# Aggregating both tiles of a pair in one run over four PSUM banks, in a four-layer graph network

## The chip, the cores and the metric

The kernel runs on one core of a Trainium2 chip. The metric is device time in microseconds (us) of the whole program, lower is better. Engines: TensorE (PE), VectorE (DVE), ScalarE (ACT), GpSimd (POOL), and SyncE (SP), which here only issues DMAs. Each engine runs its own instructions in order; semaphores order them against each other.

## What is computed

`x` is 128 graphs of 64 nodes with 512 features, fp32. Each of four layers ends in `x = layernorm(x + layer(x))`. The change is in layer 1, a graph attention with four heads, an output attention and a feed-forward part:

```python
Wh = einsum('bnf,hfo->bhno', x, W_heads)                       # 4 heads, 512 -> 512
e = leaky(Wh . a[:, :O] (i)  +  Wh . a[:, O:] (j));  attn = softmax(where(adj > 0, e, -1e9))
h = elu(einsum('bhnm,bhmo->bhno', attn, Wh))  -> [b, n, 4 * 512]
out = elu(the same attention with one head, W_out [2048, 512])
y = layernorm(relu(out @ w1 + b1) @ w2 + b2 + out)
```

## The kernel before

Two graphs make a tile of 128 rows, two tiles (j = 0, 1) a pair; layer 1 takes 32 pairs. Large products are done in three passes on fp32r halves (hi and lo). The node sums come first, the weights after: for two heads at a time (q = 0, 1) PE aggregates, `agg = xa^T x attention` (`aggregate`, L2031: sixteen matmul records of 64 rows, one graph in each half of the array), ACT copies the hi half out of PSUM (`y_hi`, L1440), DVE the lo half (`y_lo`, L1737), PE projects head h (`project`, L2048, 48 matmuls into `hp`), ACT and DVE make elu (`exp` L1447, `elu` L1745 and L1748) and split it (`h_hi` L1452, `h_lo` L1754), and PE adds the head's share of the output weights into `wop` (`out_part`, L2062, 24 matmuls a head, four parts c).

Two attentions go beside it. `at` is the head attention of the next pair's tiles 2p+2 and 2p+3. Its vectors f are 8 dot products a tile: POOL multiplies (`products_of`, L1293, through only two buffers), ACT sums (`dots`, L1432). POOL makes a diagonal (`pool_diag`, L203 the large step), PE spreads it (`pe_scores`, L212), DVE does five steps (`dve_before_exp`, L221 to L234), ACT the exponential (L241), DVE `dve_after_exp`, POOL the probabilities (`pool_prob`, two parts of L254), PE turns them (`pe_turn`, L262), ACT copies (`act_turned`). `ao` is the output attention of the pair before (m = p - 1): `keep_wo` (ACT, L1460) takes `wop` out of PSUM, `out_f` (DVE, L1768 and L1772) makes two sums, POOL the diagonal (L93), then scores (PE, L101), DVE, ACT, DVE, `pool_prob`, `pe_turn` (L148), `out_sums` (L2070), `out_exp`, `out_elu` (L1778, L1781), `split_att` (ACT L1472, POOL L1298 and L1303), `natural` (DVE, L1790) and stores by SP.

PSUM has eight banks: `agg` two, `hp` two, `wop` two, `smallp` and `shared` one each; the last two hold the small products of both attentions. There is one diagonal buffer for the heads, so `pool_diag` of a tile waits until the scores of the tile before are done:

```python
pool.wait_ge(self.f_ready[j], 8 * p + HEADS)
ge(pool, self.scores_done, t)
```

The order on every engine is written out by hand in one `step(p)` for each. PE's before is: `project` 0, `out_part(m,3)` c 0 and 1, `aggregate(p,1,0)`, c 2 and 3, `project` 1, `at` turn 2p+2, `out_part(p,0)` 0 and 1, `ao` scores 2m, `aggregate(p,1,1)`, 2 and 3, `at` scores 2p+3, `project` 2, `ao` turn 2m, `out_part(p,1)` 0 and 1, `at` turn 2p+3, 2, `ao` scores 2m+1, 3, `out_sums` 2m, `aggregate(p+1,0,0)`, `project` 3, `ao` turn 2m+1, `out_part(p,2)` 0 and 1, `aggregate(p+1,0,1)`, 2 and 3, `out_sums` 2m+1, `at` scores 2p+4.

Of the kernel before, what the change touches and what calls it, by code (L numbers as in the profile page):

```python
# [160 lines left out]
class HeadAttention:  # L161
# [55 lines left out]
    def dve_before_exp(self, nc, dve, t, p, j, fill):  # L217
        dve.wait_ge(self.scores_done, t + 1)
# [4 lines left out]
                                ).then_inc(self.summed, 1)  # L223
        dve.wait_ge(self.summed, t + 1)
# [185 lines left out]
def gnn_stack_kernel(nc, x, x_turned, adj, W0T, b0, Wh, ah, Wo, ao, w1, b1, w2, b2, gamma, beta,  # L410
# [17 lines left out]
    with ExitStack() as top:  # L428
# [520 lines left out]
        with ExitStack() as ctx:  # L949
# [32 lines left out]
            smallp = pb("smallp", [P, D])  # L982
            shared = pb("shared", [P, D])
# [151 lines left out]
            def _(sp):  # L1135
# [40 lines left out]
                def step(p):  # L1176
                    if pair(p - 2):
                        store(2 * p - 3, 1)
# [3 lines left out]
                    if fresh(p + 2) and later(p):  # L1182
                        load_dots(2 * p + 4)
# [93 lines left out]
            def _(pool):  # L1277
# [30 lines left out]
                def step(p):  # L1308
                    m = p - 1
                    if pair(p + 1):  # L1310
                        if later(p):
                            products_of(2 * p + 3, p + 1, 1, range(2, 4))
                        at.pool_prob(nc, pool, 2 * p + 2)
                        if later(p):
                            products_of(2 * p + 3, p + 1, 1, range(4, 5))
                    if pair(p - 2):
                        split_att(2 * (p - 2) + 1, 1)
                    if pair(p + 1):
                        if later(p):
                            products_of(2 * p + 3, p + 1, 1, range(5, 6))  # L1320
                        at.pool_diag(nc, pool, 2 * p + 3, p + 1, 1, i64)
                        if later(p):
                            products_of(2 * p + 3, p + 1, 1, range(6, 7))
                    if pair(m):
                        ao_.pool_diag(nc, pool, 2 * m, i64)
                    if pair(p + 1):
                        if later(p):
                            products_of(2 * p + 3, p + 1, 1, range(7, NV))
                    if fresh(p + 2):
                        products_of(2 * p + 4, p + 2, 0, range(0, 2))  # L1330
                    if pair(m):
# [90 lines left out]
            def _(act):  # L1422
# [890 lines left out]
```

## Time and profile before

| | us |
|---|---|
| median of 3 runs (3083.88 to 3086.51) | 3086.3 |
| profiled execution, whole | 3088.17 |
| its span, first to last instruction | 3086.5 |

The comparison is by the median; rows of the trace add up to the span, 1.7 us less than the profiled execution's own time.

### The profile page before, as it was taken

The numbers are of one execution on the slowest core, as the hardware profiler recorded it, in microseconds if no ns is written. First come the engines' busy times: TensorE is split into PE (matmuls) and PEld (weight loads), VectorE is DVE, ScalarE is ACT, GpSimd is POOL, SyncE is SP. The second block draws the span as 40 slices with busy tenths as digits, with TensorE's granted clock in tenths as the row PEclk, the third lists the DMA queues.
The fourth block names the chain that finished last, engine by engine and source line by source line (L and its number), as shares of the span: only waits on it lengthen the run. The fifth ranks groups of instructions, "written<-read, shape, count | busy, mean of one in ns | idle before, by whom it ended". The sixth has DMA issues, their size and how long they took to land.

```text
span 3086.5 us, 65234 instructions
## 1 busy us (share of the span) xinstructions
PE 3025.1 (98%) x19324; PEld 2655.5 (86%) x19324; DVE 2321.6 (75%) x4877; ACT 1726.6 (56%) x4250; POOL 2120.1 (69%) x2901
## 2 busy tenths in 40 slices
PE   8999989999999999999999999999799999999997
PEld 7888878888998988888889888898688888888885
DVE  7777646777777777777777777675788888888885
ACT  3333335555555555555555555553577677776675
POOL 5666645666676666667666666651588888888885
PEclk9999989999999999999999999999999999999999
DMA  5555421112111111211111111112623333233220
GB/s 201 181 187 177 154 83 32 52 44 54 38 54 48 51 51 44 54 38 54 48 48 54 44 50 42 54 45 71 189 90 102 93 101 94 89 99 102 92 75 32
DMA packets 308643, 247.65 MB, mean 80 GB/s; under 512 B 150060, under 2 KB 215644, under 8 KB 308316
## 3 DMA queue, kind: packets, MB, share of 16 engines
q1 hardware_dynamic: 296796, 221.64, 24.1%
q10 hardware_dynamic: 9216, 16.78, 1.4%
q0 software_dynamic: 2560, 8.39, 0.8%
q8 instruction: 32, 0.52, 0.1%
q14 instruction: 39, 0.32, 0.0%
HBM read 162.83 MB, written 83.91 MB: 80 GB/s over the span
## 4 chain that ended last, share of the span: by engine, by line
PE 79%; issue 3%; POOL 3%; DVE 1%; DMA 0%; ACT 0%; SPq 0%; POOLq 0%; DVEq 0%; ACTq 0%
PE hp L2048 24%; PE wop L2062 23%; PE wop L47 9%; PE hp L2188 5%; PE hp L47 5%; PE agg L2031 5%; PE shared L2070 2%; PE shared L2155 2%; PE agg L2155 2%; PE shared L262 1%; POOL g_terms L1361 1%; POOL cols L403 0%; PE smallp L212 0%; PE smallp L101 0%; POOL x1b L1374 0%
## 5 line engine op out<-in xcount | busy, mean ns | idle before, releaser
L1293 POOL TENSOR_TENSOR w_first<-xd,v_row 128x512 f32<-128x512 f32 x480 | 690.9, 1452 | 351.1 <-DMA xd<-x_scratch 275.8
L2048 PE MATMUL hp<-yT_hi,big_hi 128*128 128x256 f32 x2048 | 583.7, 285 | 1.4 <-DVE yT_lo L1737 1.4
L2048 PE MATMUL hp<-yT_hi,big_lo 128*128 128x256 f32 x2048 | 580.7, 284 | 0.0
L2048 PE MATMUL hp<-yT_lo,big_hi 128*128 128x256 f32 x2048 | 580.4, 283 | 0.0
L2062 PE MATMUL wop<-big_hi,hT_hi 128*128 128x512 f32 x1024 | 424.7, 415 | 0.0
L1754 DVE TENSOR_TENSOR hT_lo<-ex,hT_hi 128x512 fp32r<-128x512 f32 x256 | 258.6, 1010 | 200.9 <-ACT hT_hi L1452 198.3
L2062 PE MATMUL wop<-big_hi,hT_lo 128*128 128x512 f32 x1024 | 401.5, 392 | 0.0
L2062 PE MATMUL wop<-big_lo,hT_hi 128*128 128x512 f32 x1024 | 400.0, 391 | 0.0
L2048 PEld LDWEIGHTS hp<-yT_hi,big_hi 128*128 128x128 f32 x2048 | 393.5, 192 | 6.8 <-DVE yT_lo L1737 1.7
L2048 PEld LDWEIGHTS hp<-yT_lo,big_hi 128*128 128x128 f32 x2048 | 393.6, 192 | 1.2
L2048 PEld LDWEIGHTS hp<-yT_hi,big_lo 128*128 128x128 f32 x2048 | 393.6, 192 | 0.0
L1432 ACT ACTIVATE w_first<-w_first 128x512 f32<-128x512 f32 x480 | 301.6, 628 | 121.1 <-POOL w_first L1293 121.1
L1361 POOL TENSOR_TENSOR g_terms<-x,g_v_row 128x512 f32<-128x512 f32 x256 | 342.3, 1358 | 35.2 <-ACT x L1613 35.2
L1737 DVE TENSOR_TENSOR yT_lo<-agg,yT_hi 128x512 fp32r<-128x512 f32 x256 | 176.3, 689 | 202.2 <-ACT yT_hi L1440 199.0
L1440 ACT CAST yT_hi<-agg 128x512 fp32r<-128x512 f32 x256 | 149.8, 585 | 262.8 <-PE agg L2031 131.1
L2062 PEld LDWEIGHTS wop<-big_hi,hT_lo 128*128 128x128 f32 x1024 | 192.2, 188 | 43.4
L2062 PEld LDWEIGHTS wop<-big_hi,hT_hi 128*128 128x128 f32 x1024 | 192.5, 188 | 42.2
L47 PE MATMUL wop<-w_hi,g_agg_hi 128*128 128x512 f32 x512 | 219.3, 428 | 4.7 <-DVE g_agg_lo L1879 4.5
L2062 PEld LDWEIGHTS wop<-big_lo,hT_hi 128*128 128x128 f32 x1024 | 193.2, 189 | 31.9
L1447 ACT ACTIVATE ex<-hp 128x512 f32<-128x512 f32 x256 | 152.9, 597 | 109.2 <-PE hp L2048 108.1
L47 PE MATMUL wop<-w_hi,g_agg_lo 128*128 128x512 f32 x512 | 202.3, 395 | 0.0
L47 PE MATMUL wop<-w_lo,g_agg_hi 128*128 128x512 f32 x512 | 201.3, 393 | 0.0
(215 smaller groups left out, 8009.2 us busy)
## 6 DMA issues: line engine op xcount, KB each, us to landing
x0f<-in_x_turned SPq DMA_DIRECT2D x64, 256.0 KB, 2.7
xt<-in_x SPq DMA_DIRECT2D x64, 256.0 KB, 3.0
x_scratch<-w_first ACTq DMA_DIRECT2D x64, 256.0 KB, 2.3
xa<-x_scratch SPq DMA_DIRECT2D x64, 256.0 KB, 2.7
att_hi_scratch<-att_hi SPq DMA_DIRECT2D x64, 256.0 KB, 2.0
att_lo_scratch<-who SPq DMA_DIRECT2D x64, 256.0 KB, 2.0
att_hi<-att_hi_scratch SPq DMA_DIRECT2D x64, 256.0 KB, 3.6
att_lo<-att_lo_scratch SPq DMA_DIRECT2D x64, 256.0 KB, 4.3
```

Source lines behind the costliest of these rows:

```text
L47: ins = nc.tensor.matmul(out, a, b, start=first and c == 0 and q == 0, stop=last and c == n - 1 and q == 2)
L1293: nc.gpsimd.tensor_tensor(terms[:, k % TR, :], xd[:], v_row[:, k, :], ALU.mult).then_inc(terms_ready, 1)
L1361: nc.gpsimd.tensor_tensor(g.terms[:, k, :], x, g.v_row[:, k, :], ALU.mult).then_inc(g.terms_ready, 1)
L1432: nc.scalar.activation(terms[:, k % TR, :], terms[:, k % TR, :], ACT.Identity, accum_out=at.f[:, j, k:k + 1]).then_inc(at.f_ready[j], 1)
L1440: nc.scalar.copy(yT[0][:, side, :, own].rearrange("p c (g n) -> p g c n", g=2), agg[:].rearrange("p g (h c n) -> p h g c n", h=2, c=KC)[:, ...
L1447: nc.scalar.activation(ex[half][:], hp[half][:], ACT.Exp).then_inc(ex_ready, 1)
L1737: nc.vector.tensor_tensor(yT[1][:, side, :, own].rearrange("p c (g n) -> p g c n", g=2), agg[:].rearrange("p g (h c n) -> p h g c n", h=2, ...
L1754: nc.vector.tensor_tensor(hT[1][:, own, :].rearrange("p c n -> p (c n)"), ex[half][:], hT[0][:, own, :].bitcast(F32).rearrange("p c n -> p ...
L2031: ins = nc.tensor.matmul(by_head(agg[:, g, :])[:, :, c, :], xa[j][own, c * P:(c + 1) * P], at.turned[own, j, 2 * q:2 * q + 2, :], start=Tr ...
L2048: ins = nc.tensor.matmul(hp[half][:, s * 2 * P:(s + 1) * 2 * P], a, b, start=c == 0 and i == 0, stop=c == KC - 1 and i == 2)
L2062: ins = nc.tensor.matmul(wop[j][:], a, b, start=h == 0 and c == 0 and i == 0, stop=h == HEADS - 1 and c == KC - 1 and i == 2)
L2188: ins = nc.tensor.matmul(bank[:, s * 2 * P:(s + 1) * 2 * P], x, y, start=c == 0 and q == 0, stop=c == KC - 1 and q == 2)
```

## The change

`smallp` and `shared` become the two banks of one tile `agg_b`. `aggregate` now does both tiles of a pair in one run, tile 0 into `agg` and tile 1 into `agg_b`. Before the second half PE waits until the small results in `agg_b` have been read, and `banks_free` makes it wait for all four `y_lo` before the next small product. The small products stand in the gaps between runs, the scores of the output attention between the halves of `project`, which is split. All orders are rewritten: on POOL and ACT the products and dots of tiles 2p+4 and 2p+5 are both made in step p (before: 2p+3 and 2p+4), `dve_before_exp` of tile 2p+3 is split in two, and SP loads for the dots earlier. The diff, shortened: indentation is cut, "..." stands for removed lines of the old orders and for unchanged bodies.

```diff
@@ -215,12 +215,18 @@
         ins.then_inc(self.scores_done, 1)
     def dve_before_exp(self, nc, dve, t, p, j, fill):
+        self.dve_add(nc, dve, t, p, j)
+        self.dve_peak(nc, dve, t, fill)
+    def dve_add(self, nc, dve, t, p, j):
...
+    def dve_peak(self, nc, dve, t, fill):
         dve.wait_ge(self.summed, t + 1)
         nc.vector.scalar_tensor_tensor(self.e1, self.e1, SLOPE_L1, self.e1, ALU.mult, ALU.max
                            ).then_inc(self.leaky, 1)
@@ -979,8 +985,10 @@
 agg = pb("agg", [P, 2, D])
 hp = [pb(f"hp{b}", [P, D]) for b in range(2)]
 wop = [pb(f"wop{j}", [P, D]) for j in range(2)]
-smallp = pb("smallp", [P, D])
-shared = pb("shared", [P, D])
+agg_b = pb("agg_b", [P, 2, D])
+shared, smallp = agg_b[:, 0, :], agg_b[:, 1, :]
+banks = (agg, agg_b)
+EVICTED = ((0, 0), (1, 0), (0, 1), (1, 1))
 SO, SH, ST = NODES, P, 3 * P
 at.prob = sb("ah_prob", [P, HEADS, 2, NODES])
 at.scores_psum = smallp[:, SH:SH + HEADS * NODES]
@@ -1174,22 +1182,21 @@
                          ).then_inc(att_stored, 16)
     def step(p):
+        if fresh(p + 2) and later(p):
+            load_dots(2 * p + 4)
         if pair(p - 2):
+            store_natural(2 * p - 4, 0)
             store(2 * p - 3, 1)
         for j in range(2):
             if pair(p) and pair(p + 1):
                 load_agg(p, j)
-        if fresh(p + 2) and later(p):
-            load_dots(2 * p + 4)
+        if fresh(p + 2):
+            load_dots(2 * p + 5)
         if isinstance(p, int) and p == PAIRS - 1:
             sp.wait_ge(at.prob_ready, T)
             sp.dma_start(w_first[:], chunked(w1)).then_inc(w_first_loaded, 16)
         if pair(p - 1):
             store_halves(2 * p - 2, 0)
-        if fresh(p + 2):
-            load_dots(2 * p + 5)
-        if pair(p - 1) and not (isinstance(p, int) and p == PAIRS - 1):
-            store_natural(2 * p - 2, 0)
@@ -1307,47 +1314,44 @@
     def step(p):
         m = p - 1
+        first = 2 * p + 4, p + 2, 0
+        second = 2 * p + 5, p + 2, 1
         if pair(p + 1):
...
+            at.pool_diag(nc, pool, 2 * p + 3, p + 1, 1, i64)
+        if fresh(p + 2):
+            products_of(*first, range(0, 1))
         if pair(p - 2):
             split_att(2 * (p - 2) + 1, 1)
+        if fresh(p + 2):
+            products_of(*first, range(1, 2))
         if pair(p + 1):
...
+            at.pool_prob(nc, pool, 2 * p + 2)
+        if fresh(p + 2):
+            products_of(*first, range(2, 4))
         if pair(m):
             ao_.pool_diag(nc, pool, 2 * m, i64)
...
         if fresh(p + 2):
...
+            products_of(*first, range(4, 6))
         if pair(m):
             ao_.pool_prob(nc, pool, 2 * m)
+        if fresh(p + 2):
+            products_of(*first, range(6, NV))
+        if pair(p + 2):
+            at.pool_diag(nc, pool, 2 * p + 4, p + 2, 0, i64)
+        if pair(m):
+            ao_.pool_diag(nc, pool, 2 * m + 1, i64)
         if pair(p + 1):
             at.pool_prob(nc, pool, 2 * p + 3)
         if fresh(p + 2):
...
+            products_of(*second, range(0, 2))
         if pair(m):
             ao_.pool_prob(nc, pool, 2 * m + 1)
         if fresh(p + 2):
...
+            products_of(*second, range(2, 5))
         if pair(m):
             split_att(2 * m, 0)
...
+        if fresh(p + 2):
+            products_of(*second, range(5, NV))
@@ -1432,13 +1436,15 @@
-    def y_hi(p, q, j, side):
+    def y_hi(p, q, n):
+        j, side = EVICTED[n]
         act.wait_ge(agg_done, 4 * p + 2 * q + j + 1)
         ge(act, h_done, 2 * (4 * p + 2 * q + side - 1))
-        ge(act, y_lo_ready, 2 * (4 * p + 2 * q + j) + side)
+        if n > 1:
+            act.wait_ge(y_lo_ready, 4 * (2 * p + q) + n - 1)
         own = slice(j * P, (j + 1) * P)
         nc.scalar.copy(yT[0][:, side, :, own].rearrange("p c (g n) -> p g c n", g=2),
-                       agg[:].rearrange("p g (h c n) -> p h g c n", h=2, c=KC)[:, side]
+                       banks[j][:].rearrange("p g (h c n) -> p h g c n", h=2, c=KC)[:, side]
                        ).then_inc(y_hi_ready, 1)
@@ -1474,122 +1480,90 @@
     def step(p):
         m = p - 1
         k = 4 * p
...
+        first = 2 * p + 4, p + 2, 0
+        second = 2 * p + 5, p + 2, 1
         if pair(m):
             h_hi(k - 1, 1)
         if pair(p - 2):
             out_exp(2 * (p - 2) + 1)
...
+        exp(k, 0)
         if pair(p + 1):
             at.act_exp(nc, act, 2 * p + 2)
...
+        if fresh(p + 2):
+            dots(*first, (0,))
         if pair(p - 2):
             split_att(2 * (p - 2) + 1, 1, p - 1)
...
+        exp(k, 1)
+        h_hi(k, 0)
+        if fresh(p + 2):
+            dots(*first, (1, 2))
+        if pair(m):
+            keep_wo(m, 0)
+        h_hi(k, 1)
+        if pair(m):
+            keep_wo(m, 1)
+        if fresh(p + 2):
+            dots(*first, (3,))
+        exp(k + 1, 0)
+        if fresh(p + 2):
+            dots(*first, (4,))
+        if pair(m):
+            ao_.act_exp(nc, act, 2 * m)
+        exp(k + 1, 1)
+        for n in range(3):
+            y_hi(p, 1, n)
         if pair(p + 1):
...
+            at.act_exp(nc, act, 2 * p + 3)
+        y_hi(p, 1, 3)
+        h_hi(k + 1, 0)
+        if fresh(p + 2):
+            dots(*first, (5, 6))
+        h_hi(k + 1, 1)
         if pair(p + 1):
             at.act_turned(nc, act, 2 * p + 2, p + 1, 0, agg_done)
...
         if pair(m):
             ao_.act_turned(nc, act, 2 * m)
         if fresh(p + 2):
...
+            dots(*first, (7,))
+        exp(k + 2, 0)
+        if pair(m):
+            ao_.act_exp(nc, act, 2 * m + 1)
+        if fresh(p + 2):
+            dots(*second, (0,))
...
@@ -1731,12 +1705,13 @@
 @block.vector
 def _(dve):
-    def y_lo(p, q, j, side):
-        dve.wait_ge(y_hi_ready, 2 * (4 * p + 2 * q + j) + side + 1)
+    def y_lo(p, q, n):
+        j, side = EVICTED[n]
+        dve.wait_ge(y_hi_ready, 4 * (2 * p + q) + n + 1)
         own = slice(j * P, (j + 1) * P)
         nc.vector.tensor_tensor(
             yT[1][:, side, :, own].rearrange("p c (g n) -> p g c n", g=2),
-            agg[:].rearrange("p g (h c n) -> p h g c n", h=2, c=KC)[:, side],
+            banks[j][:].rearrange("p g (h c n) -> p h g c n", h=2, c=KC)[:, side],
             yT[0][:, side, :, own].bitcast(F32).rearrange("p c (g n) -> p g c n", g=2),
             ALU.subtract).then_inc(y_lo_ready, 1)
@@ -1798,72 +1773,54 @@
             natural(2 * (p - 2), 0)
         if pair(p + 1):
             at.dve_before_exp(nc, dve, 2 * p + 2, p + 1, 0, fill1)
...
         if pair(p - 2):
             out_elu(2 * (p - 2) + 1)
+        elu(k, 0)
         if pair(p + 1):
             at.dve_after_exp(nc, dve, 2 * p + 2)
...
+        elu(k, 1)
+        h_lo(k, 0)
+        if pair(p + 1):
+            at.dve_add(nc, dve, 2 * p + 3, p + 1, 1)
         if pair(m):
             out_f(2 * m, 0)
         if pair(p - 2):
             natural(2 * (p - 2) + 1, 1)
...
+        h_lo(k, 1)
         if pair(m):
             ao_.dve_before_exp(nc, dve, 2 * m, fill1)
...
+        elu(k + 1, 0)
+        if pair(p + 1):
+            at.dve_peak(nc, dve, 2 * p + 3, fill1)
         if pair(m):
             ao_.dve_after_exp(nc, dve, 2 * m)
...
+        elu(k + 1, 1)
+        for n in range(4):
+            y_lo(p, 1, n)
+        h_lo(k + 1, 0)
+        if pair(m):
+            out_f(2 * m + 1, 1)
         if pair(p + 1):
             at.dve_after_exp(nc, dve, 2 * p + 3)
...
+        h_lo(k + 1, 1)
+        elu(k + 2, 0)
         if pair(m):
             ao_.dve_before_exp(nc, dve, 2 * m + 1, fill1)
...
+        elu(k + 2, 1)
+        if pair(m):
+            ao_.dve_after_exp(nc, dve, 2 * m + 1)
             out_elu(2 * m)
...
+        h_lo(k + 2, 0)
+        h_lo(k + 2, 1)
+        elu(k + 3, 0)
+        elu(k + 3, 1)
         if pair(p + 1):
...
+            for n in range(4):
+                y_lo(p + 1, 0, n)
+        h_lo(k + 3, 0)
+    for n in range(4):
+        y_lo(0, 0, n)
     dve.wait_ge(a_loaded, 16)
     run(dve, step, first=0)
@@ -2021,33 +1978,40 @@
 @block.tensor
 def _(pe):
...
+    def aggregate(p, q, before):
+        a = 2 * p + q
+        for j in range(2):
+            pe.wait_ge(at.turned_ready, 2 * (2 * p + j + 1))
+            pe.wait_ge(xa_loaded[j], 16 * p + 16)
+            ge(pe, y_lo_ready, 4 * a - 1 + j)
+            if j == 1:
+                before()
...
+            ins.then_inc(agg_done, 1)
+    def banks_free(p, q):
+        pe.wait_ge(y_lo_ready, 4 * (2 * p + q) + 4)
+    def project(p, h, half):
         k = 4 * p + h
         side = h % 2
...
+        if half == 0:
+            pe.wait_ge(y_lo_ready, 4 * (2 * p + h // 2) + 2 + 2 * side)
+        ge(pe, hv_ready, 2 * (k - 1) + half + 1)
...
@@ -2073,79 +2037,72 @@
     def step(p):
         m = p - 1
...
+        def scores_read():
+            pe.wait_ge(at.summed, capped(2 * p + 4, T))
+            if pair(m):
+                ge(pe, att_ready, 2 * (p - 2) + 2)
+                pe.wait_ge(ao_.summed, 2 * m + 1)
+        def turned_read():
+            if pair(m):
+                pe.wait_ge(ao_.turned_ready, 2 * (2 * m + 2))
+        project(p, 0, 0)
+        project(p, 0, 1)
+        if pair(m):
+            for c in range(KC):
+                out_part(m, 3, c)
         if pair(p + 1):
...
+            at.pe_scores(nc, pe, 2 * p + 3, same_graph)
+        project(p, 1, 0)
+        if pair(m):
+            pe.wait_ge(at.summed, capped(2 * p + 4, T))
+            ao_.pe_scores(nc, pe, 2 * m, same_graph)
+        project(p, 1, 1)
+        aggregate(p, 1, scores_read)
+        for c in range(KC):
+            out_part(p, 0, c)
+        banks_free(p, 1)
+        if pair(p + 1):
             at.pe_turn(nc, pe, 2 * p + 2, ident)
...
+        if pair(m):
             ao_.pe_turn(nc, pe, 2 * m, ident)
...
+        project(p, 2, 0)
+        if pair(m):
+            pe.wait_ge(ao_.turned_ready, 2 * (2 * m + 1))
+            ao_.pe_scores(nc, pe, 2 * m + 1, same_graph)
+        project(p, 2, 1)
+        if pair(m):
+            pe.wait_ge(at.turned_ready, capped(2 * (2 * p + 3), 2 * T))
+            out_sums(2 * m, 0)
+        for c in range(KC):
+            out_part(p, 1, c)
+        if pair(m):
+            pe.wait_ge(ao_.summed, 2 * m + 2)
+            ao_.pe_turn(nc, pe, 2 * m + 1, ident)
+            pe.wait_ge(att_ready, 2 * m + 1)
         if pair(p + 1):
             at.pe_turn(nc, pe, 2 * p + 3, ident)
...
+        project(p, 3, 0)
+        project(p, 3, 1)
         if pair(p + 1):
...
+            aggregate(p + 1, 0, turned_read)
+        for c in range(KC):
+            out_part(p, 2, c)
         if pair(p + 1):
...
+            banks_free(p + 1, 0)
+        if pair(m):
             out_sums(2 * m + 1, 1)
         if pair(p + 2):
...
             at.pe_scores(nc, pe, 2 * p + 4, same_graph)
...
+    def nothing_before():
+        pass
+    aggregate(0, 0, nothing_before)
+    banks_free(0, 0)
     at.pe_scores(nc, pe, 2, same_graph)
...
     run(pe, step, first=0)
```

## Rows read from the trace of the kernel before

**Rows 1.** The page's busy table: us (share of the span), instructions.

```profile
PE 3025.1 (98%) x19324; PEld 2655.5 (86%) x19324; DVE 2321.6 (75%) x4877; ACT 1726.6 (56%) x4250; POOL 2120.1 (69%) x2901
```

**Rows 2.** Windows, layer 1: length, busy us of PE, PEld, DVE, ACT, POOL; granted clock.

```profile
431.70:2140.00 1708.30, 1706.91 (x12175) 1533.19 (x12175) 1246.31 (x2306) 953.23 (x2335) 1100.13 (x1093) 1.00 0.17 47
```

**Rows 3.** The chain that ended last: start us, us, what.

```profile
1002.37 5.95 PE hp L2048 x48
...
1056.34 5.95 PE hp L2048 x48
```

**Rows 4.** Timeline of PE around one aggregation run.

```profile
1010.57 0.39 PE L2062 MATMUL wop<-big_lo,hT_hi 128*128 128x512 f32 x1
1010.79 0.39 PE L2062 MATMUL wop<-big_hi,hT_lo 128*128 128x512 f32 x1
1011.11 1.16 PE L2031 MATMUL agg<-ah_turned,xa 64*128 64x128 f32 x16
1012.20 0.50 PE L2062 MATMUL wop<-big_hi,hT_hi 128*128 128x512 f32 x1
1012.54 0.39 PE L2062 MATMUL wop<-big_lo,hT_hi 128*128 128x512 f32 x1
```

**Rows 5.** The run's first four matmuls: ns shortest/median/longest, start us.

```profile
L2031 PE MATMUL agg<-ah_turned,xa x4: 272/322/373, 1011.1 to 1011.3; 64*128 64x128 f32 x4
```

**Rows 6.** Timeline of PE: project 1 behind out_part(m,3), and the ao scores.

```profile
1028.72 0.28 PE L2048 MATMUL hp<-yT_hi,big_hi 128*128 128x256 f32 x1
...
1037.66 0.33 PE L101 MATMUL smallp<-ao_diag,same_graph 128*128 128x64 f32 x2
```

**Rows 7.** Timelines of ACT and DVE behind out_part(m,3).

```profile
1029.06 0.59 ACT L1460 COPY who<-wop 128x512 f32<-128x512 f32 x1 [1.71 <-PE wop L2062]
...
1030.81 0.69 DVE L1768 CUSTOM_DVE_ANT_0 att_hi<-who,ao_row 128x512 f32<-128x512 f32 x1
...
1032.27 0.71 DVE L1790 STREAM_TRANSPOSE att_hi<-attT 128x512 f32<-128x512 f32 x1
```

**Rows 8.** Source lines on POOL and ACT, 700:1700 us: ns shortest/median/longest.

```profile
L1293 POOL TENSOR_TENSOR w_first<-xd,v_row x294: 1264/1302/1845, 701.0 to 1693.8; 128x512 f32<-128x512 f32 x147
...
L1298 POOL TENSOR_TENSOR who<-attT,att_hi x37: 1272/1737/1754, 702.3 to 1675.8; 128x512 fp32r<-128x512 f32 x37
...
L1303 POOL TENSOR_TENSOR attT<-attT,b_col x37: 1040/1042/1042, 704.1 to 1677.6; 128x512 f32<-128x512 f32 x37
...
L254 POOL TENSOR_TENSOR ah_prob<-w_first,ah_inv x76: 609/638/1064, 699.8 to 1699.6; 128x256 f32<-128x256 f32 x76
...
L93 POOL TENSOR_TENSOR ao_diag<-i,ao_f x37: 291/478/486, 710.3 to 1683.9; 128x64 f32<-128x64 f32 x37
...
L1432 ACT ACTIVATE w_first<-w_first x295: 614/628/647, 702.8 to 1697.7; 128x512 f32<-128x512 f32 x148
```

**Rows 9.** Timeline of DVE: steps of both attentions, h_lo, y_lo, elu.

```profile
1002.74 1.53 DVE L1754 TENSOR_TENSOR hT_lo<-ex,hT_hi 128x512 fp32r<-128x512 f32 x1
...
1040.44 0.21 DVE L109 TENSOR_TENSOR ao_e<-smallp,ao_f 128x64 f32<-128x64 f32 x1
...
1041.41 0.68 DVE L1754 TENSOR_TENSOR hT_lo<-ex,hT_hi 128x512 fp32r<-128x512 f32 x1
1042.01 0.68 DVE L1737 TENSOR_TENSOR yT_lo<-agg,yT_hi 128x512 fp32r<-128x512 f32 x1
...
1043.47 0.41 DVE L221 TENSOR_TENSOR w_first<-smallp,ah_f 128x256 f32<-128x256 f32 x1
...
1046.30 0.52 DVE L1745 TENSOR_SCALAR ex<-ex 128x512 f32<-128x512 f32 x1
1046.85 0.69 DVE L1748 TENSOR_TENSOR ex<-hp,ex 128x512 f32<-128x512 f32 x1
```

**Rows 10.** Timeline of POOL beside the first row of rows 9.

```profile
1002.68 1.05 POOL L203 TENSOR_TENSOR ah_diag<-i,ah_f_halves 128x512 fp32r<-128x512 f32 x1
```

**Rows 11.** Windows, near the kernel's end, same columns.

```profile
3053.00:3060.00 7.00, 4.85 (x23) 4.09 (x22) 2.44 (x7) 3.24 (x9) 2.57 (x4) 0.76 0.00 1
```

More of the change, by code:

```diff
@@ L1516, in step @@
-                    if pair(p + 1):
-                        if later(p):
-                            dots(*d1, (5,))
-                    if pair(p):
-                        y_hi(p, 1, 0, 1)
+                    if fresh(p + 2):
[6 more added lines that the diff above has]
+                    exp(k + 1, 1)
@@ L1553, in step @@
+                    h_hi(k + 2, 0)
+                    if pair(m):
+                        split_att(2 * m, 0, m + 1)
+                    if fresh(p + 2):
+                        dots(*second, (2, 3))
+                    h_hi(k + 2, 1)
                     if pair(p + 1):
                         at.act_turned(nc, act, 2 * p + 3, p + 1, 1, agg_done)
-                    if pair(p):
-                        h_hi(k + 2, 0)
-                    if fresh(p + 2):
-                        dots(*d0, (3,))
@@ L1581, in step @@
+                    exp(k + 3, 1)
                     if pair(p + 1):
-                        y_hi(p + 1, 0, 1, 0)
-                    if pair(p):
-                        h_hi(k + 3, 0)
+                        for n in range(3):
+                            y_hi(p + 1, 0, n)
+                    if fresh(p + 2):
+                        dots(*second, (6,))
                     if pair(p + 1):
-                        y_hi(p + 1, 0, 1, 1)
+                        y_hi(p + 1, 0, 3)
+                    h_hi(k + 3, 0)
@@ L1587, in step @@
                     if fresh(p + 2):
-                        dots(*d0, (7,))
-                for j in range(2):
-                    for side in range(2):
-                        y_hi(0, 0, j, side)
+                        dots(*second, (7,))
+                for n in range(4):
+                    y_hi(0, 0, n)
                 run(act, step, first=0)
@@ L1855, in step @@
-                    if pair(p):
-                        elu(k + 3, 1)
-                    if pair(p + 1):
-                        y_lo(p + 1, 0, 1, 0)
-                    if pair(p):
-                        h_lo(k + 3, 0)
-                    if pair(p + 1):
-                        y_lo(p + 1, 0, 1, 1)
-                for j in range(2):
-                    for side in range(2):
-                        y_lo(0, 0, j, side)
+                        for n in range(4):
+                            y_lo(p + 1, 0, n)
@@ L2036, in project @@
-                def project(p, h):
+                def aggregate(p, q, before):
[7 more added lines that the diff above has]
+                        for c in range(KC):
+                            for g in range(2):
+                                own = slice(g * NODES, (g + 1) * NODES)
+                                ins = nc.tensor.matmul(by_head(banks[j][:, g, :])[:, :, c, :],
+                                                       xa[j][own, c * P:(c + 1) * P],
+                                                       at.turned[own, j, 2 * q:2 * q + 2, :], start=True, stop=True)
+                        ins.then_inc(agg_done, 1)
```

229 lines of the change are left out of this document (23 added, 206 removed).

## Prediction

> **What bounds the kernel now.** I read the page's busy table first: PE works 98% of the span [rows 1]. The windows sharpen it for layer 1: from 431.7 to 2140 us PE is busy 1706.9 of 1708.3 us, at full granted clock, DVE 1246 (73%), ACT 953, POOL 1100 (64%) [rows 2]. So inside layer 1 time is saved only by making PE's own stream shorter, and is lost by anything that makes PE wait. The chain that ended last gives the pair's length: project 3 of one pair starts at 1002.37 and of the next at 1056.34, 53.97 us [rows 3].
>
> **What the change removes: two entries and two exits of aggregation runs a pair.** PE's timeline [rows 4] shows what a run of 16 half-height matmuls costs besides itself. Products into `wop` start every 0.23 us; the run starts 0.32 after the last one, so 0.09 extra. The next product starts at 1012.20 and its successor at 1012.54, 0.34 later, 0.11 extra. Inside, the first two matmuls take 0.373 and the next 0.272 [rows 5], 0.10 extra. The last pair starts at 1011.11 + 1.16 - 0.27 = 1012.00 and the product follows 0.20 later, while inside the run a pair follows a pair after (0.89 - 0.10)/7 = 0.11: 0.09 extra. That is 0.39 a run. Today there are four runs a pair, after the change two of double length: 2 x 0.39 = 0.79 us saved. What bounds this: nothing if the second half, which goes to other banks, pays entry again; 0.79 if not. I take 0.79, since pairs of matmuls inside a run already alternate between two banks at 0.11.
>
> The small products (transposes, scores, sums) are as many as before and stand among the same two kinds of large products, so I let them keep their price. That leaves -0.79 a pair if PE never waits; over 31 pairs that have both attentions, -24 us.
>
> **What it adds: waits with less room.** Let a pair begin (t = 0) when project 0 starts, right behind the head scores of tile 2p+2. Without waits PE is at: project 0 until 5.75, all four `out_part(m,3)` until 11.25, head scores 11.5, half of project 1 at 14.36, and there `ao_.pe_scores(2m)`. Today these scores stand 8.9 us behind the end of `out_part(m,3)` (1028.72 to 1037.66 [rows 6]); afterwards 3.11 us (0.24 for the head scores, half of 5.75). Behind that end comes a chain on three engines: ACT's `keep_wo` starts 0.33 later and takes 0.59, DVE's two sums of `out_f` take 1.46 together (1030.81 to 1032.27), POOL's `ao` diagonal 0.29 to 0.48, about 0.1 of hand-overs [rows 7, 8]. 2.85 us at best, 3.4 with the medians: 0.26 of room, or a stall of 0.3, even if all three engines are free on the instant.
>
> They are not. ACT has `dots(first, (1, 2))` ahead of `keep_wo`, and dot 2 needs POOL's product 2 of the new tile. POOL stands at the head of the step in `pool_diag(2p+3)`, which needs the scores of tile 2p+2 done, thus t = 0.2. Its queue from there, by the shortest durations of [rows 8]: diagonal 1.6 (two small steps with their gaps, then 1.05 [rows 10]), product 0 1.3, then `split_att`, which waits for ACT's split of the output tile. That one comes when DVE has done `h_lo`, `natural`, the five steps of `dve_before_exp` and `out_elu`: from -0.25 (ACT's `h_hi` ends there, `out_part` having ended at -1.1), 0.6 + 0.63 + 2.3 + 1.15 [rows 7, 9] brings 4.4, plus 0.6 on ACT and hand-overs: 5.1. (The five steps took 2.83 from 1043.47, one of them 0.5 over its shortest; `out_elu` has the form of the pair at 1046.30.) Then 1.28 + 1.04 (split), 1.26 (product 1), 1.2 (two parts of `pool_prob`), 1.26 (product 2): 11.2. Dot 2 0.72, `keep_wo` ends at 12.55, `out_f` 14.1, diagonal and hand-over 14.5. PE stands at 14.36: 0.15 of stall by the shortest durations.
>
> Shortest is rare there. POOL and those DVE instructions that read two SBUF operands or run fast exclude each other in this trace: `h_lo` began at 1002.74 beside POOL's 1002.68 + 1.05 = 1003.73 and ended at 1004.27, 1.53 instead of 0.68 [rows 9, 10]. POOL's products run from 1.26 to 1.85, its split from 1.27 to 1.75 (median 1.74), a part of `pool_prob` from 0.61 to 1.06 [rows 8]. Walking the queue again with each collision where it falls: the `dve_before_exp` steps lose 0.8, so the split starts at 5.9; its second part loses 0.2 to `elu(k, 1)`, `pool_prob` 0.6 to `h_lo(k, 0)`; product 2 ends at 12.75, dot 2 at 13.5, `keep_wo` 14.1, `out_f` 15.6, PE goes at 16.0. Stall 1.65.
>
> The Trainium skill (SBUF — State Buffer, "SBUF: two separate sides") has this as an exclusive lock of a shared port pair, held for a whole instruction; the trace agrees (1.53 against 0.68). By it the stall is the 1.65 just given; a kernel without the lock would have 0.15.
>
> **The second room.** After project 1 comes the double run, `out_part(p,0)`, then `banks_free`, the transposes, half of project 2 and `ao_.pe_scores(2m+1)`, 14.2 us behind the first `ao` scores. In between DVE must do, in order, `natural`, `h_lo`, `ao`'s five steps, `elu`, `dve_peak`, `elu`, four `y_lo`: 0.63 + 0.6 + 0.98 + 1.07 + 1.85 + 0.1 + 1.07 + 2.44 = 8.74 from the end of `out_f` [rows 7, 9]; PE asks for the banks 11.2 after it (0.4 of diagonal, 0.22 scores, half a projection 2.88, the double run 2.2, `out_part` 5.5). Collisions take about 2 of these: `banks_free` itself just passes, stall 0 to 0.5. But the last `y_hi` on ACT stands before `h_hi(k+1,0)` and dots 5 and 6; dot 5 lets POOL's product 7 go, then the diagonal of 2p+4, then `ao`'s for 2m+1, which PE waits for. Last `y_hi` end 26.1 + 0.6 + 0.7 + 1.3 + 1.6 + 0.4 = 30.7 at the least, PE there at 30.2; with collisions (`out_f(2m+1)` runs beside it) 31.7. Stall 0.4 to 1.5. What is late then is everything behind on PE, while DVE, ACT and POOL have their slack in the second half (there I find 2 us before each wait: `banks_free` of the next pair's run at 52 against 50, the `ao` turn at 38 against 35.5).
>
> **SP's queue** gives something back: `load_dots(2p+5)` no longer stands behind `store_halves`, and `load_dots(2p+4)` is first in the step. POOL's waits for `xd` shrink. It is worth nothing on PE: POOL, done with product 7 near 46, meets the diagonal wait at the step's head instead, some 7 us.
>
> **Sum.** Stalls a pair: 0.15 + 0.4 = 0.55 by the shortest durations, 1.65 + 1.5 = 3.15 with every collision. Medians lie at both ends of their spreads (product 1.30 of 1.26 to 1.85, split 1.74 of 1.27 to 1.75 [rows 8]), so I take the middle, 1.85. -0.79 + 1.85 = +1.06 a pair, x 31 = +33 us. The profiled execution took 3088.2, 1.9 over the median shown, so 3088.2 + 33 - 1.9 = 3119 us. The ends: -0.24 x 31 = -7 (3079) and +2.36 x 31 = +73 (3159). No term for start and tail: first pair and the stages after layer 1 keep their order but for one store.
>
> **Rivals.** (1) As above, PE waits for the `ao` diagonals, over 1.0 us a pair: 3093 to 3159, chance 0.60. (2) The chains hold: my walk puts POOL too late by a microsecond or more, for instance if ACT's split finds `att_ready` at 3.5 rather than 4.5, and both stalls vanish; then the merged runs alone count: -24 us, 3062, up to 3079 with the shortest stalls. The place is dot 2 against `keep_wo`: it decides if product 2 ends before 10.9. For it: every engine but PE is idle over a quarter of layer 1 [rows 2], and POOL waits less for loads. Against: POOL's queue starts anew at each t = 0. Chance 0.25. (3) Merged runs save and stalls cost alike, within 0.2% (6 us, about what this measurement can tell): stalls of 0.6 to 1.0, chance 0.10. (4) The stall also costs the clock. Near the kernel's end, where PE is busy 4.85 of 7 us, the mean granted clock is 0.76 over those 7 us [rows 11]; with the levels 2.4 and 1.2 GHz that is 0.48 x 7 = 3.4 us at the lower one, 1.7 us lost. In each pair that is +53 on top, about 3170. Against it: my stalls are under 2 us each and stand in dense work. Chance 0.05.
>
> **Numbers.** Likeliest 3119, its own range 3093 to 3159. For 8 in 10 it takes in most of (2) and nearly all of (1): 3066 to 3159. Faster 0.25, same 0.10, slower 0.65.
>
> **What would show it.** PE's `agg` groups of 32 with 0.32 before and 0.34 behind, once each. PE idle before L101 (`ao` scores) on POOL's L93, twice a pair, 0.3 to 1.7 each; `keep_wo` ending over 1 us after `out_part(m,3)` ended, behind an L1432. If PE stays at 99% of layer 1 and pairs last 53.2, rival 2. If the wait is on `y_lo` at the transposes, my DVE sum is too small. If runs of 32 take over 2.2 us, the saving is not there.

## The result and the profile after

| | us |
|---|---|
| before, median of its 4 runs (3083.88 to 3086.51) | 3085.89 |
| after, median of 4 runs (3117.14 to 3119.13) | 3117.77 |
| ratio after to before, 95% interval | 1.0105, 1.0088 to 1.0123 |
| span of the profiled execution after (before 3086.5) | 3115.4 |

The kernel is 32 us, 1.05%, slower. First the windows of layer 1, the same stretch as in [rows 2]; the columns are length, then busy time of PE, PE's weight loads, DVE, ACT, POOL, then the granted clock, the DMA share and GB/s:

```profile
431.70:2140.00 1708.30, 1654.58 (x11940) 1505.46 (x11940) 1170.58 (x2263) 953.51 (x2309) 1048.13 (x1082) 1.00 0.16 46
```

PE was busy 1706.9 of these 1708.3 us before and is busy 1654.6 now, at full granted clock. It lost 53.7 us of work by waiting. The list of waits of layer 1 in the kernel after (engine, line, what it waited for: us in all, times, longest) names the place; the same list before has one wait of PE, of 0.3 us:

```profile
POOL ah_f_halves L196 <- PE agg_b L212: 240.7, 30, 8.3
PE agg_b L101 <- POOL ao_diag L93: 29.3, 28, 1.1
PE agg_b L101 <- issue: 24.4, 28, 0.9
```

Both of PE's are the scores of the output attention, once for tile 2m and once for 2m+1, in 28 pairs. "Issue" means that PE's matmul had no releaser that the profile shows; its diagonal had just ended, as the rows further down show. POOL's 8 us are its wait for the head scores at the start of the step.

PE's timeline around the merged run, after (start, duration, line, operation; a count at the end, idle time before in brackets), answers to [rows 4]:

```profile
1014.86 0.28 PE L2012 MATMUL hp<-yT_hi,big_lo 128*128 128x256 f32 x1
1015.06 1.16 PE L1992 MATMUL agg<-ah_turned,xa 64*128 64x128 f32 x16
1016.06 1.06 PE L1992 MATMUL agg_b<-ah_turned,xa 64*128 64x128 f32 x16
1017.05 0.50 PE L2026 MATMUL wop<-big_hi,hT_hi 128*128 128x512 f32 x1
1017.38 0.39 PE L2026 MATMUL wop<-big_lo,hT_hi 128*128 128x512 f32 x1
...
1039.28 0.43 PE L101 MATMUL agg_b<-ao_diag,same_graph 128*128 128x64 f32 x2 [1.05 <-POOL ao_diag L93]
...
1054.57 0.41 PE L101 MATMUL agg_b<-ao_diag,same_graph 128*128 128x64 f32 x2 [0.86 <-issue]
```

The second half of the run (1016.06) starts 1.00 after the first and pays no entry again; `wop` products follow at 1017.05 and 1017.38, 0.33 apart, once for 32 matmuls. The next pair's run starts at 1070.52, so this pair lasts 55.46 against 53.97 [rows 3]. Two stalls, 1.05 and 0.86, stand in it.

**The first stall, followed back.** Project 0 starts at 1023.76 (t = 0 of the prediction). The chain that ended last, of the kernel after (start, duration, what), runs through POOL's and ACT's work and returns to PE at the scores:

```profile
1026.59 2.09 DMA att_scratch<-who
1028.68 0.63 ACT att_hi L1478
...
1029.38 1.30 POOL who L1305
...
1031.83 1.29 POOL w_first L1300
...
1034.67 2.54 POOL w_first L1300 x2
1037.21 1.69 issue
1038.93 0.30 POOL ao_diag L93
1039.28 0.43 PE agg_b L101 x2
```

The pair of products that begins at 1034.67 holds product 2, the one dot 2 waits for. ACT's and DVE's timelines of the kernel after:

```profile
1035.99 0.63 ACT L1436 ACTIVATE w_first<-w_first 128x512 f32<-128x512 f32 x1 [2.11 <-POOL w_first L1300]
...
1036.62 0.57 ACT L1466 COPY who<-wop 128x512 f32<-128x512 f32 x1
```

```profile
1037.42 0.69 DVE L1743 CUSTOM_DVE_ANT_0 att_hi<-who,ao_row 128x512 f32<-128x512 f32 x1 [1.59 <-ACT who L1466]
...
1038.16 0.69 DVE L1747 CUSTOM_DVE_ANT_0 att_hi<-who,ao_row 128x512 f32<-128x512 f32 x1
```

ACT had stood idle 2.11 us for product 2 when `keep_wo` (L1466) could have begun at 1035.3, an estimate: 0.33 behind the start of the PE work that follows `out_part(m,3)` (1034.97), as in [rows 6, 7].

**The second stall.** ACT's timeline of the kernel after, then POOL's:

```profile
1048.23 0.58 ACT L1446 CAST yT_hi<-agg_b 128x512 fp32r<-128x512 f32 x1
1048.69 0.63 ACT L1458 CAST hT_hi<-ex 128x512 fp32r<-128x512 f32 x1
1049.21 0.65 ACT L1436 ACTIVATE w_first<-w_first 128x512 f32<-128x512 f32 x1
```

```profile
1050.02 1.28 POOL L1300 TENSOR_TENSOR w_first<-xd,v_row 128x512 f32<-128x512 f32 x1 [2.30 <-ACT w_first L1436]
1051.27 0.65 POOL L196 TENSOR_TENSOR ah_f_halves<-ah_f,ones 128x4 fp32r<-128x4 f32 x1
...
1052.73 1.04 POOL L203 TENSOR_TENSOR ah_diag<-i,ah_f_halves 128x512 fp32r<-128x512 f32 x1
1053.73 0.74 POOL L93 TENSOR_TENSOR ao_diag<-i,ao_f 128x64 f32<-128x64 f32 x1
```

Last `y_hi`, `h_hi`, dot 5, product 7, the head diagonal of 2p+4, and only then the small `ao` diagonal, which ends at 1054.47, 0.1 before PE goes on.

### The profile page after: what moved, and what is told of

It is laid out like the page before. It is cut to its first block, busy times and chain, and to the rows that moved or that the text cites. A ratio compares the mean times of both kernels' runs of the same rounds, so it can differ in the third digit from the quotient of the medians.

```text
span 3115.4 us, 65262 instructions
## 1 busy us (share of the span) xinstructions
PE 3003.0 (96%) x19324; PEld 2656.3 (85%) x19324; DVE 2262.0 (73%) x4877; ACT 1737.4 (56%) x4250; POOL 2070.8 (66%) x2901
## 4 chain that ended last, share of the span: by engine, by line
PE 65%; POOL 8%; issue 7%; DMA 2%; SPq 1%; DVE 1%; ACT 1%; POOLq 0%; DVEq 0%; ACTq 0%
PE wop L2026 18%; PE hp L2012 16%; PE wop L47 9%; PE hp L2145 5%; PE hp L47 5%; POOL w_first L1300 3%; PE agg L1992 2%; PE agg_b L1992 2%; DMA att_scratch<-who 2%; PE agg_b L2034 2%; PE agg_b L2112 2%; PE agg L2112 2%; SPq L1181 1%; POOL who L1305 1%; POOL g_terms L1365 1%
## 5 line engine op out<-in xcount | busy, mean ns | idle before, releaser
L1300 POOL TENSOR_TENSOR w_first<-xd,v_row 128x512 f32<-128x512 f32 x480 | 637.8, 1344 | 88.2 <-ACT w_first L1436 88.2
L1729 DVE TENSOR_TENSOR hT_lo<-ex,hT_hi 128x512 fp32r<-128x512 f32 x256 | 269.8, 1054 | 229.8 <-ACT hT_hi L1458 229.7
L2026 PE MATMUL wop<-big_hi,hT_hi 128*128 128x512 f32 x1024 | 408.3, 399 | 0.0
L1458 ACT CAST hT_hi<-ex 128x512 fp32r<-128x512 f32 x256 | 158.9, 621 | 213.7 <-PE wop L2026 213.7
L1720 DVE TENSOR_SCALAR ex<-ex 128x512 f32<-128x512 f32 x256 | 125.5, 490 | 192.8 <-ACT ex L1453 191.3
```

Of the source, the lines that this page charges most:

```text
L1300: nc.gpsimd.tensor_tensor(terms[:, k % TR, :], xd[:], v_row[:, k, :], ALU.mult).then_inc(terms_ready, 1)
L1458: nc.scalar.copy(hT[0][:, 2 * half:2 * half + 2, :].rearrange("p c n -> p (c n)"), ex[half][:]).then_inc(hT_hi_ready, 1)
L1720: nc.vector.tensor_scalar(ex[half][:], ex[half][:], 1.0, -1.0, ALU.min, ALU.add).then_inc(neg_ready, 1)
L1729: nc.vector.tensor_tensor(hT[1][:, own, :].rearrange("p c n -> p (c n)"), ex[half][:], hT[0][:, own, :].bitcast(F32).rearrange("p c n -> p ...
L2026: ins = nc.tensor.matmul(wop[j][:], a, b, start=h == 0 and c == 0 and i == 0, stop=h == HEADS - 1 and c == KC - 1 and i == 2)
```

## Experiments

Each is compared with the kernel before, run beside it (medians 3087.21, 3085.64 and 3086.15 us in the three batches). Line numbers of experiments can differ from those of after by 2. The theory was that the two stalls, each on one `ao` diagonal, hide a real saving of the merged runs. The expectations speak of stalls of 1.20 and 1.02 where the profile has 1.05 and 0.86 of idle time: the record of a product into `hp` lasts 0.28 but the next one normally starts 0.12 behind it, so the first 0.16 of a wait leaves no idle time.

**e1: keep_wo ahead of dot 2 (ACT).**

```diff
-                        dots(*first, (1, 2))
+                        dots(*first, (1,))
                     if pair(m):
                         keep_wo(m, 0)
+                    if fresh(p + 2):
+                        dots(*first, (2,))
```

> ACT takes dot 2 behind keep_wo instead of ahead of it; nothing else moves. Theory (the first stall, 1.20 us a pair before the output attention's scores of tile 2m, is keep_wo held up by dot 2): keep_wo starts 1.3 us earlier, but out_f now falls beside POOL's product 3 and loses up to 1 us to it, so the first stall falls to between 0.2 and 1.0 us, the second stays near 1.0; 3088 to 3112 us. Rival A (the four y_lo in a row and banks_free set the pair): no change, 3118. Rival B (POOL as a whole is too late, ACT's order does not matter): no change, 3118.

Measured: 3108.75 us, ratio 1.0066 (1.0049 to 1.0083). The first stall shrinks from 1.05 to 0.69 and stays. `keep_wo` is early now, but `out_f` falls beside POOL's products. DVE's timeline of e1, then POOL's:

```profile
1032.29 1.64 DVE L1745 CUSTOM_DVE_ANT_0 att_hi<-who,ao_row 128x512 f32<-128x512 f32 x1 [0.29 <-ACT who L1466]
```

```profile
1030.84 2.54 POOL L1300 TENSOR_TENSOR w_first<-xd,v_row 128x512 f32<-128x512 f32 x2
```

The sum takes 1.64 beside the products and 0.69 alone. `keep_wo` starts 1.32 us earlier in the pair (11.54 instead of 12.86 behind the start of project 0), 0.95 of that is lost at the sum, and 0.36 is left, the part by which the stall shrinks. So dot 2 alone does not cure it: product 3 takes most of the gain back.

**e2, e3, e4: POOL's order.** e2 makes products 0 and 1 of the new tile before the head diagonal, in POOL's idle time at the head of the step; e3 puts the `ao` diagonal ahead of the head diagonal of 2p+4; e4 does both.

```diff
@@ e2 @@
+                    if fresh(p + 2):
+                        products_of(*first, range(0, 2))
                     if pair(p + 1):
                         at.pool_diag(nc, pool, 2 * p + 3, p + 1, 1, i64)
-                    if fresh(p + 2):
-                        products_of(*first, range(0, 1))
                     if pair(p - 2):
                         split_att(2 * (p - 2) + 1, 1)
-                    if fresh(p + 2):
-                        products_of(*first, range(1, 2))
@@ e3 @@
-                    if pair(p + 2):
-                        at.pool_diag(nc, pool, 2 * p + 4, p + 2, 0, i64)
                     if pair(m):
                         ao_.pool_diag(nc, pool, 2 * m + 1, i64)
+                    if pair(p + 2):
+                        at.pool_diag(nc, pool, 2 * p + 4, p + 2, 0, i64)
```

> POOL makes products 0 and 1 of the new tile before it waits for the scores at the head of the step, in its 8 us of idle time there. Theory: product 2 ends some 2.5 us earlier, dot 2 no longer holds keep_wo, product 3 is done before out_f begins; the first stall falls from 1.20 to 0.0 to 0.2 us, the second stays at 1.0; 3118 - 29 x 1.1 = 3086, 3080 to 3094. Rival A (y_lo and banks_free): no change, 3118. Rival B (POOL's total work is too much): no change, since its work is the same.

> POOL makes the output attention's diagonal of tile 2m+1 before the head diagonal of tile 2p+4; two lines change places. Theory: the diagonal then waits only for out_f and stands 1.1 us earlier; the second stall falls from 1.02 to 0 to 0.2 us, the first stays at 1.20: 3118 - 29 x 0.9 = 3092, 3086 to 3100. Rival A: no change, 3118. Rival C (what is late is the chain y_hi, h_hi, dot 5, product 7 and the diagonal order only adds its last bit): half the stall goes, 3103.

> The edits of the two kernels before together. Theory (the two stalls are independent, and the double run does save 0.75 us a pair): pairs of 53.2 to 53.5 us, 3118 - 29 x 2.1 = 3057, 3052 to 3070, under both the kernel before (3086) and after. Rival A: 3118. Rival D (the room is used up elsewhere: removing two stalls brings PE to the next wait, y_lo at banks_free, sooner): 3075 to 3095, with PE waiting on y_lo before the transposes.

Measured: e2 3083.82 us (0.9985, 0.9975 to 0.9995), e3 3086.42 us (0.9995, 0.9986 to 1.0005), e4 3051.04 us (0.9879, 0.9862 to 0.9895). PE's waits at the `ao` scores in layer 1, e2 first, then e3:

```profile
PE agg_b L101 <- issue: 25.8, 28, 1.0
```

```profile
PE agg_b L101 <- POOL ao_diag L93: 29.3, 28, 1.1
```

Each order removes one stall and leaves the other nearly as it was (25.8 us for 24.4 in e2, 29.3 for 29.3 in e3). In e4, 1 us under the range expected, one wait of 0.8 us at the scores is left in all of layer 1; PE's timeline of e4 at the first scores and the next two runs:

```profile
1018.15 0.34 PE L101 MATMUL agg_b<-ao_diag,same_graph 128*128 128x64 f32 x2
1018.30 0.36 PE L2010 MATMUL hp<-yT_hi,big_hi 128*128 128x256 f32 x1
...
1021.34 1.16 PE L1990 MATMUL agg<-ah_turned,xa 64*128 64x128 f32 x16
...
1074.38 1.16 PE L1990 MATMUL agg<-ah_turned,xa 64*128 64x128 f32 x16
```

The pair lasts 53.04: PE's own work. Behind a stall the scores cost 0.24 to the next product (1039.28 to 1039.52), here 0.15. Behind the second stall they cost 0.22. So a pair of after is 53.04 + 1.05 + 0.86 of idle time + 0.16 at the entry of each stall, which the records hide, + 0.09 and 0.07 behind them = 55.43, against 55.46 measured, and the stalls cost 2.40 a pair. 28 x 2.40 = 67 us; after less e4 is 66.7. e4 beats the kernel before by 36 us and the one after by 67. (e4 and after were run in different batches, in which the kernel before had 3087.2 and 3085.9.)

**e5: dots 1, 2 and 3 all ahead of keep_wo, to make the first stall longer.**

```diff
-                        dots(*first, (1, 2))
+                        dots(*first, (1, 2, 3))
...
-                    if fresh(p + 2):
-                        dots(*first, (3,))
```

> The suspected cost doubled, on the changed kernel: ACT takes dot 3 as well as dots 1 and 2 ahead of keep_wo. Dot 3 needs POOL's product 3, which ends 1.25 us after product 2. Theory: keep_wo starts 1.2 to 1.3 us later and the first stall grows from 1.20 to 2.4 us; the second keeps its size, since its chain starts behind the first: 3118 + 29 x 1.2 = 3153, 3140 to 3156. Rival B (POOL as a whole is late, ACT's order does not matter): 3118. Rival D (the first stall shortens the second by what it grows): 3118 to 3125.

Measured: 3167.56 us, 1.0264 (1.0246 to 1.0281), above the range expected. PE's timeline of e5 and the window behind the stall (the clock is third from the end):

```profile
1060.23 0.47 PE L101 MATMUL agg_b<-ao_diag,same_graph 128*128 128x64 f32 x2 [2.30 <-POOL ao_diag L93]
...
1060.82 0.42 PE L2010 MATMUL hp<-yT_lo,big_hi 128*128 128x256 f32 x1
1061.03 0.41 PE L2010 MATMUL hp<-yT_hi,big_lo 128*128 128x256 f32 x1
```

```profile
1060.50:1063.90 3.40, 3.40 (x18) 3.40 (x18) 3.29 (x8) 0.83 (x3) 2.59 (x2) 0.50 0.33 58
```

Idle for 2.30 us, and then the granted clock is 0.50, the lower of the two levels, for 3.4 us. Products of `hp` start every 0.21 instead of 0.12. It happened behind this stall in 20 of 28 pairs and not in 8. In those 20 the second stall is gone, since PE comes later by itself; in the 8 it is there with 0.86 to 0.88. So the clock costs only 0.45 a pair: 57.16 us with it (547.08 to 604.24) and 56.71 without (604.24 to 660.95). The expectation had the longer stall, 28 x 1.25 = 35 us, and not the clock, 20 x 0.45 = 9 us. That makes 3162; of the 6 us left, 5.4 are the first pair of layer 1, which lasts 50.95 for 45.53 in after, and why is open.

**e6 and e7: the merged run split again,** the first quarter of `out_part` between its halves; e6 on e4, e7 on the kernel after.

```diff
                         if j == 1:
+                            if between:
+                                between()
                             before()
...
-                    aggregate(p, 1, scores_read)
-                    for c in range(KC):
+                    aggregate(p, 1, scores_read, lambda: out_part(p, 0, 0))
+                    for c in range(1, KC):
                         out_part(p, 0, c)
```

(and the same at the run of `q` 0 of the next pair.)

> The stall-free kernel (both POOL orders) with each double run split in two by the six products of out_part c = 0, so that there are four runs a pair again, all else as it is. Theory (0.39 us for each entry and exit of a run): 0.79 us more a pair, 3051 + 31 x 0.79 = 3075, 3071 to 3080. Rival E (entry and exit cost nothing; the gain of the stall-free kernel comes from the order of the small products): 3051. Rival F (the second bank pair pays its own entry anyway): 3051 to 3055.

> The same split on the changed kernel with its two stalls. Theory: the run of q = 1 stands between the two stalls, where DVE and ACT set the pace and PE waits 1.0 us, so its 0.39 is swallowed by the second stall; the run of the next pair stands where PE sets the pace and costs its 0.39: 3118 + 31 x 0.39 = 3130, 3126 to 3134. Rival (both on the path): 3142. Rival E or F: 3118.

Measured: e6 3079.23 us (0.9979, 0.9969 to 0.9989), e7 3134.08 us (1.0158, 1.0141 to 1.0175). PE's timeline of e6:

```profile
1002.80 0.28 PE L2012 MATMUL hp<-yT_hi,big_lo 128*128 128x256 f32 x1
1003.01 1.16 PE L1992 MATMUL agg<-ah_turned,xa 64*128 64x128 f32 x16
1004.10 0.50 PE L2026 MATMUL wop<-big_hi,hT_hi 128*128 128x512 f32 x1
1004.44 0.39 PE L2026 MATMUL wop<-big_lo,hT_hi 128*128 128x512 f32 x1
...
1005.37 0.40 PE L2026 MATMUL wop<-big_hi,hT_lo 128*128 128x512 f32 x1
1005.69 1.16 PE L1992 MATMUL agg_b<-ah_turned,xa 64*128 64x128 f32 x16
```

Each half now enters and leaves by itself: the first starts 0.21 behind a product into `hp`, which come every 0.12, the second 0.32 behind one into `wop`, which come every 0.23; behind the first the next two products stand 0.34 apart. The pair is 53.94 (1003.01 to 1056.95) instead of 53.04, 0.44 a run, and the kernel 28.2 us longer. e7 is only 16.3 longer than after, at the upper edge of its range. PE's waits in layer 1 of e7 show where the rest went:

```profile
PE agg_b L101 <- POOL ao_diag L93: 29.5, 28, 1.1
PE agg_b L101 <- issue: 12.3, 28, 0.6
```

The second stall fell from 24.4 to 12.3 in all: PE does the extra 0.44 of the run ahead of it where it would have waited.

**e8: the second ao scores behind all of project 2,** on the kernel after, to see how much room stands behind them.

```diff
                         pe.wait_ge(ao_.turned_ready, 2 * (2 * m + 1))
-                        ao_.pe_scores(nc, pe, 2 * m + 1, same_graph)
                     project(p, 2, 1)
                     if pair(m):
+                        ao_.pe_scores(nc, pe, 2 * m + 1, same_graph)
```

> The changed kernel with the scores of tile 2m+1 behind the whole of project 2 instead of between its halves, 2.9 us later on PE; POOL and ACT untouched. Theory: the diagonal is ready 1.0 us after the old place, so the second stall goes; the chain to the turn of 2m+1 had over 2 us of room and loses 1.9: 3118 - 29 x 1.0 = 3089, 3086 to 3098. Rival (the room behind is smaller than worked out: the stall moves to the turn behind out_part(p,1)): 3095 to 3118 with PE waiting for ao_prob.

Measured: 3103.68 us, 1.0060 (1.0043 to 1.0077), above the 3086 to 3098 expected. PE's waits in layer 1 of e8, then its timeline in one pair:

```profile
PE agg_b L2034 <- DVE yT_lo L1712: 10.7, 28, 0.4
PE agg_b L101 <- POOL ao_diag L93: 28.6, 28, 1.1
```

```profile
1072.53 1.15 PE L2034 MATMUL agg_b<-ao_turned,who 128*128 128x128 f32 x8 [0.37 <-DVE yT_lo L1712]
```

The second stall is gone, but the work of DVE and ACT that hangs on these scores came later against PE, and PE met `banks_free` of the next pair's run with 0.37 of new idle time. Moving a request later costs room elsewhere; moving the work earlier (e3) cost nothing.

**e9: e1, with the ao diagonal behind product 2 instead of behind product 3** on POOL.

```diff
-                        products_of(*first, range(2, 4))
+                        products_of(*first, range(2, 3))
                     if pair(m):
                         ao_.pool_diag(nc, pool, 2 * m, i64)
                     if fresh(p + 2):
-                        products_of(*first, range(4, 6))
+                        products_of(*first, range(3, 6))
```

> The changed kernel with dot 2 behind keep_wo (as in the first experiment) and, on POOL, the output attention's diagonal of tile 2m ahead of product 3, so that POOL stands idle while out_f runs. In the first experiment the first sum of out_f took 1.64 us beside product 3 instead of 0.69. Theory (the two engines exclude each other): out_f takes 1.5 us in all, the diagonal is ready 0.2 us before PE asks, the first stall goes; the second stays near 1.0, or grows a little because dot 3 and the exponential behind it come 1.3 us later: 3108.8 - 29 x 0.85 = 3084, 3082 to 3100. Rival (out_f took long for a reason of its own, such as its read of the accumulator or ACT's write): 3100 to 3109.

Measured: 3097.20 us, 1.0037 (1.0023 to 1.0052). DVE's timeline of e9, and PE's waits in layer 1:

```profile
1030.05 0.69 DVE L1745 CUSTOM_DVE_ANT_0 att_hi<-who,ao_row 128x512 f32<-128x512 f32 x1 [0.29 <-ACT who L1466]
...
1030.78 0.69 DVE L1749 CUSTOM_DVE_ANT_0 att_hi<-who,ao_row 128x512 f32<-128x512 f32 x1
```

```profile
PE agg_b L101 <- issue: 39.2, 29, 1.4
```

With POOL idle beside them both sums are back at 0.69 and the first stall is gone, which settles what e1 left. POOL spent 1.7 us idle for it, product 7 and both diagonals behind it came later, and the second stall grew from 0.86 to 1.37. e2, which spends POOL's idle time at the head of the step, is the better cure: 3083.8 us.

## Why the prediction was right

**The mechanism.** Rival 1 came as told: PE waits for the `ao` diagonals, twice a pair, and pays more than the merged runs save. Rival 2 (the chains hold) did not come; e4 shows what it would have been, 3051 instead of 3062. Rival 3 (savings and stalls alike) did not come either: 67 us were paid for 36. Rival 4 (the clock lost as well) did not come with idles of 1.05 and 0.86 us: granted clock 1.00 in layer 1. e5 shows its place: with 2.30 us of idle it comes in 20 of 28 pairs, though at 0.45 a pair and not 1.7, because the next stall absorbs most of it.

**The number was luck.** 3117.8 was measured for 3119 forecast, but both terms were too small, and the errors offset each other. Stalls: 1.85 a pair taken, the middle between two bounds, over 31 pairs, 57 us; 2.40 measured over 28 pairs, 67 us. Savings: 24 us taken, 36 by e4 against before.

**What the savings are made of.** Entry and exit of a run are 0.44 by e6 against e4 for the 0.39 taken, 28 us. Some 6 more are the difference of e6 from the kernel before (3079.2 against 3085.6), though both have four runs a pair. The 1.6 that are missing to 36 are what the kernel before differs by between the two batches (3087.2 and 3085.6). The pair of [rows 3], 53.97, is the usual one before and hardly differs from the 53.93 of e6. But of 30 pairs before (from 460.50 to 2084.91), 11 last 54.46 to 54.54, such as the one whose first run starts at 1055.17 and the next pair's at 1109.66. 11 x 0.54 = 6 us. In these pairs PE waits for POOL in the kernel before too. PE's timeline and then POOL's, of before:

```profile
1104.89 0.65 PE L262 MATMUL shared<-ident,ah_prob 128*128 128x128 f32 x4
...
1106.99 0.41 PE L101 MATMUL smallp<-ao_diag,same_graph 128*128 128x64 f32 x2
```

```profile
1103.13 1.63 POOL L254 TENSOR_TENSOR ah_prob<-w_first,ah_inv 128x256 f32<-128x256 f32 x2 [2.74 <-DVE ah_inv L248]
...
1106.42 0.47 POOL L93 TENSOR_TENSOR ao_diag<-i,ao_f 128x64 f32<-128x64 f32 x1
```

The transposes start 0.13 behind the end of `ah_prob` and 0.41 behind the last product, the scores 0.10 behind the end of `ao_diag` and 0.45 behind the last product; in all 18 pairs of usual length both stand 0.23 behind the last product, with POOL done 0.6 us or more before. A product into `wop` has a record of 0.39 and the next starts 0.23 behind it, so such waits leave almost no idle time in the profile: PE looked 99.9% busy. The prediction took the kernel before to be free of waits and read one pair for all. In e6 every pair but the first lasts 53.92 to 53.95. Which of the new places saves these waits was not tried alone, nor what makes POOL late in some pairs before and not in others.

**The first room.** Predicted: split at t = 5.1 to 5.9, product 2 done at 11.2 to 12.75, `keep_wo` done at 12.55 to 14.1, PE at 14.5 to 16.0. Measured: 5.6, 12.2, 13.4, 15.5. Every step lies in its range. (The shortest chain behind `out_part(m,3)` adds up to 2.77 from its rows, not 2.85; nothing hangs on it.) One cause was missing: ACT's split waited last for the DMA that stores the natural layout (`att_scratch<-who`, 2.09 us, done at 1028.68), not for `out_elu`, because the change moved that store to the head of SP's step; the prediction looked only at the loads for the dots there. It cost ACT's split 0.1 us: ACT's own queue was busy until 1028.56.

**The exclusion of DVE and POOL.** Expected as 1.53 against 0.68; seen again at `out_f`: 1.64 in e1 beside products, 0.69 in e9 with POOL idle, and 1.81 at the first sum of tile 2m+1 in the kernel after, beside product 7. The Trainium skill (SBUF — State Buffer, "SBUF: two separate sides") calls it an exclusive lock for a whole instruction; e1 against e9 agrees.

**The second room.** `banks_free` "just passes": the last `y_lo` ended at 1049.53 and PE's transposes began at 1050.13, 0.6 later. The chain over dot 5 and product 7 came step by step, and e3 shows that it is the head diagonal in front of the `ao` diagonal that makes it late: it holds POOL from 1051.27 to 1053.73, and PE had run out of work at 1053.71. The time at which the diagonal was ready, 30.7, was met by two errors: the last `y_hi` ended at 25.05 for the 26.1 of the working, and what follows took 5.66 for 4.6, of which the head diagonal 2.46 for 1.6.

**The room behind the stalls.** I had found 2 us before each wait in the second half. For the kernel after that holds: its last `y_lo` ended at 1020.10, PE asked at 1022.62. For e8 I carried it over and took 1.9 off it, and it did not hold. Against the rest of PE's work the scores came a whole half projection, 2.9 us, later, since PE no longer loses the stall; that is 0.4 more than the 2.5 there were, and 0.37 was measured.

**What would show it.** Of the list, the runs of 32 with one entry and one exit, L101 idle twice a pair, and `keep_wo` late behind an ACT dot are all there. The entry shows as 0.20 and not 0.32, because a product into `hp` (every 0.12) now stands in front and not one into `wop` (every 0.23).

## What to carry to other kernels

When the bound engine's own stream is shortened or its small jobs are packed together, write down for each job the moment it asks and the moment its operand is ready, with every instruction queued ahead on each engine in between; the gain here (36 us) was real and was lost twice over (67 us) to two queue places. Both stalls here were cured by order alone: put the operation that the bound engine waits for ahead of work with slack, and use an engine's idle time earlier in the step, before moving the request later. Read the length of a period over many periods, not from one, and compare starts: where the records of an engine overlap, a short wait leaves no idle time.

## What the runs showed of the hardware

- Entering and leaving a run of 64-row matmuls among full-height ones costs 0.44 us a run: 0.89 a pair for four runs of 16 instead of two of 32 (e6 against e4).
- A pair of matmuls of 128x64 takes 0.22 or 0.24 to the next product's start behind a stall, 0.15 without a stall before it (after against e4).
- Idle times of 1.05 us (after) and 1.37 us (e9) amid dense work left the granted clock at 1.00. Of 28 idle times of 2.30 us (e5), 20 were followed by 3.4 us at 0.50 and 8 by none.
